# A layer handover rearranged at five places: VectorE work in parts, output products between state sums, one table load placed by hand

## What is computed

```python
x = x + _L0_xattn_ref(_layernorm(x), ctx_4096, ...)  # both operands quantised to 8 bit codes, then one matmul
x = x + _L0_attn_ref(_layernorm(x), ...)             # state space layer: W_in, conv, scan, gate, W_out
x = x + _L0_ffn_ref(_layernorm(x), ...)              # W_base and a routed low-rank sum of 8 experts
x = x + _L1_xattn_ref(_layernorm(x), ctx_4096, ...)  # cross attention over 1024 context rows
x = x + _L1_attn_ref(_layernorm(x), ...)             # causal attention, 32 heads, 8 key heads
x = x + _L1_ffn_ref(_layernorm(x), ...)              # permuted columns, per-head up, GELU, down
```

## Time and profile before

| | us |
|---|---|
| median of 3 runs | 383.94 |
| lowest, highest | 383.87, 384.13 |
| profiled execution, device time | 383.87 |
| profiled execution, span of the trace | 382.1 |
| TensorE busy | 346.7 |
| VectorE busy | 271.5 |
| ScalarE busy | 199.0 |
| GpSimd busy | 121.3 |

### The profile page before, as it was taken

The page is one execution under the profiler, slowest core; times in us unless marked ns, Lnnn a source line. Parts: engine busy times, 40 slices in busy tenths (PEclk is TensorE's granted clock), DMA queues, the critical chain, the costliest instruction groups (busy, mean ns, idle before and its releaser), DMA issues.

```text
span 382.1 us, 5181 instructions
## 1 busy us (share of the span) xinstructions
PE 346.7 (91%) x1996; PEld 223.9 (59%) x1996; DVE 271.5 (71%) x352; ACT 199.0 (52%) x397; POOL 121.3 (32%) x96
## 2 busy tenths in 40 slices
PE   0688999999899989999999979799999989899996
PEld 0335444654566656566754857588443467787785
DVE  2867067757887999998975589887820699976381
ACT  1980223179999688688702664554010379252160
POOL 2600000025999888798920020201000020210000
PEclk9999999999999999999999999999999999999999
DMA  6999999563003011166137789399999997000001
GB/s 252 421 424 407 350 422 383 208 218 112 2 1 112 0 60 51 50 211 240 50 107 237 324 333 425 120 334 332 341 420 423 409 421 307 2 3 0 0 3 55
DMA packets 12967, 81.86 MB, mean 214 GB/s; under 512 B 2109, under 2 KB 2365, under 8 KB 3661
## 3 DMA queue, kind: packets, MB, share of 16 engines
q1 hardware_dynamic: 11614, 78.23, 52.9%
q10 hardware_dynamic: 1296, 3.22, 2.5%
q0 software_dynamic: 32, 0.07, 0.0%
HBM read 80.86 MB, written 0.52 MB: 213 GB/s over the span
## 4 chain that ended last, share of the span: by engine, by line
PE 63%; DVE 15%; POOL 10%; DMA 6%; ACT 3%; issue 2%; SPq 0%; DVEq 0%; ACTq 0%; POOLq 0%
PE psum L1021 13%; PE psum L973 10%; PE psum L1141 7%; PE psum L1242 6%; DMA ring<-in_ctx 6%; PE psum L1097 5%; POOL arena L620 5%; PE psum L980 5%; PE psum L935 4%; PE psum L1165 3%; DVE rounded L1646 2%; DVE arena L1603 2%; POOL arena L623 2%; PE psum L1396 2%; PE psum L1361 2%; POOL plain L620 2%
## 5 line engine op out<-in xcount | busy, mean ns | idle before, releaser
L770 ACT ACTIVATE arena<-arena 128x126 f32<-128x126 f32 x256 | 76.5, 388 | 9.8 <-DVE arena L1603 8.8
L1021 PE MATMUL psum<-ring,hT 128*128 128x512 f32 x128 | 60.6, 602 | 0.8 <-ACT hT L686 0.8
L1603 DVE TENSOR_TENSOR_SCAN arena<-arena,psum 128x1024 f32<-128x1024 f32 x24 | 54.2, 2273 | 3.3 <-PE psum L1097 3.0
L560 POOL TENSOR_TENSOR small<-small 128x1 f32<-128x1 f32 x6 | 9.3, 1553 | 133.0 <-DVE small L1446 127.4
L620 POOL TENSOR_TENSOR arena<-arena 128x1024 f32<-128x1024 f32 x20 | 47.2, 2361 | 5.4 <-DVE arena L1603 5.4
L1646 DVE TENSOR_TENSOR rounded<-ring,rounded 128x2048 fp32r<-128x2048 f32 x16 | 36.5, 2286 | 10.2 <-ACT rounded L797 10.1
L1141 PEld LDWEIGHTS psum<-arena,ident 128*128 128x128 f32 x292 | 35.6, 192 | 13.8 <-issue 10.0
L797 ACT ACTIVATE rounded<-ring 128x2048 fp32r<-128x2048 f32 x16 | 30.6, 1912 | 24.8 <-PE psum L980 15.3
L1141 PE MATMUL psum<-arena,ident 128*128 128x128 f32 x292 | 37.3, 278 | 1.5 <-POOL arena L623 1.5
L1021 PEld LDWEIGHTS psum<-ring,hT 128*128 128x128 f32 x128 | 22.2, 190 | 27.1 <-issue 26.0
L1097 PE MATMUL psum<-plain 64*128 64x512 f32 x128 | 36.1, 641 | 1.7 <-DVE arena L1603 1.4
(11 more groups left out here) (213 smaller groups left out, 581.2 us busy)
## 6 DMA issues: line engine op xcount, KB each, us to landing
ring<-in_w_in SPq DMA_DIRECT2D x16, 1024.0 KB, 14.1
ring<-in_ctx SPq DMA_DIRECT2D x13, 1024.0 KB, 11.9
ring<-in_w_out SPq DMA_DIRECT2D x8, 1024.0 KB, 4.8
ring<-in_ctx_t SPq DMA_DIRECT2D x7, 1024.0 KB, 6.4
ring<-in_w_base SPq DMA_DIRECT2D x4, 1024.0 KB, 4.8
ring<-in_x_wk SPq DMA_DIRECT2D x4, 1024.0 KB, 7.9
ring<-in_a_wo SPq DMA_DIRECT2D x4, 1024.0 KB, 10.9
ring<-in_x_wq SPq DMA_DIRECT2D x3, 1024.0 KB, 8.9
```

Of the source, the lines that this page charges most:

```text
L770: last = act.activation(to, of, ACT.Exp, scale=a_par[:, k, state_no:state_no + 1])
L1021: last = pe.matmul(psum[:, proj_bank(j), :], hT[:, k, :], slot(w_in + u)[:, k % UK, :], start=(k == 0), stop=(k == KT - 1))
L1603: dve.tensor_tensor_scan(state[s % STATES], dA[:, s % 3, :], psum[:, p:p + 2, :].rearrange("p a b -> p (a b)"), 0.0, ALU.mult, ALU.add).th ...
```

## The change

- `context_offset(0)` goes between `code(4)` and `code(5)`, `add_to_x(0, 0)` between `code(5)` and `code(6)`. In unit 7 the last two query products are issued after the last two column sums, with a signal of their own (`q_done` now counts to 3).
- `statistics(0)` goes from `add_to_x` to `variance`, in all handovers.
- `low(5)`, `low(9)`, `low(17)` become two halves (`low_part`), one ahead of `left_low` and one behind it, both ahead of `variance`.
- `low(16)` goes ahead of both `add_to_x`; on ACT `high(17)` goes ahead of `left_high(hT_psum, 8)`.
- Three `output` products stand behind each of `state_sum(29)`, `state_sum(30)`, and the rest behind the last, in place of two, two and the rest.
- The idle products ahead of the second layer's transposes are 5 instead of 11.
- ACT's table for GELU is loaded behind the last `left_high`, ahead of the copy of `picked`.

```diff
-            pool.wait_ge(q_done, 2)
+            pool.wait_ge(q_done, 3)
...
             high(16)
+            high(17)
             left_high(hT_psum, 8)
-            high(17)
             high(18)
...
             left_high(hT_psum, 10)
+            act.preload_act_table_set("gelu_and_others")
             act.wait_ge(g_psum, 1)
...
-                            pe.matmul(psum[rows, nh, :], q1T[:, UK * kh + k, rows], right, **at)
+                            if u < 7 or k < UK // 2:
+                                pe.matmul(psum[rows, nh, :], q1T[:, UK * kh + k, rows], right, **at)
                             last = pe.matmul(psum[rows, 2 + nh, :], ones64, right, **at)
                 last.then_inc(q_done, 1)
+            for k in range(UK // 2, UK):
+                last = pe.matmul(psum[L:P, 1, :], q1T[:, UK + k, L:P], q2[:, 7, UN * k:UN * k + UN], start=False,
+                                 stop=(k == UK - 1))
+            last.then_inc(q_done, 1)
...
-            idle_products(4, 11)
+            idle_products(4, 5)
             transpose_h(1)
...
             state_sum(STEPS - 3)
-            output(0, 0)
-            output(0, 1)
+            for k in range(3):
+                output(0, k)
             state_sum(STEPS - 2)
-            output(0, 2)
             output(0, 3)
+            output(1, 0)
+            output(1, 1)
             state_sum(STEPS - 1)
-            for k in range(GD):
-                output(1, k)
+            output(1, 2)
+            output(1, 3)
...
                 dve.wait_ge(x_ready, updates[0])
-                if nh == 0:
-                    statistics(0)
...
             def variance(n):
 
+                statistics(0)
                 statistics(1)
...
             code(4)
+            dve.wait_ge(x_offset, 1)
+            context_offset(0)
             code(5)
+            add_to_x(0, 0, q_s12)
             code(6)
             code(7)
-            dve.wait_ge(x_offset, 1)
-            for nh in range(2):
-                context_offset(nh)
-                add_to_x(nh, nh, q_s12)
+            context_offset(1)
+            dve.wait_ge(q_done, 3)
+            add_to_x(1, 1, q_s12)
...
+            def low_part(m, part):
+
+                dve.wait_ge(unit_high, m + 1)
+                unit = unit_halves[m % 3]
+                v = slice(2 * part, 2 * part + 2)
+                last = dve.tensor_tensor(unit[:, 1, v, :], slot(split_units[m])[:, v, :], unit[:, 0, v, :].bitcast(F32),
+                                         ALU.subtract)
+                if part:
+                    last.then_inc(unit_low, 1)
...
             center()
+            low_part(5, 0)
             left_low(2)
+            low_part(5, 1)
             variance(2)
-            low(5)
             low(6)
...
             for nh in range(2):
-                if nh == 1:
+                if nh == 0:
                     low(16)
                 dve.wait_ge(xatt_psum, nh + 1)
                 add_to_x(nh, 2 + nh, sinv)
```

More of the change, by code:

```diff
@@ L1699, in _ @@
             center()
+            low_part(9, 0)
             left_low(4)
+            low_part(9, 1)
             variance(3)
-            low(9)
             low(10)
@@ L1756, in _ @@
             center()
+            low_part(17, 0)
             left_low(6)
+            low_part(17, 1)
             variance(4)
-            low(17)
             low(18)
```

## The result

| | median us | lowest to highest | profiled execution | span |
|---|---|---|---|---|
| before | 384.01 | 383.87 to 384.13 | 383.87 | 382.1 |
| changed | 379.04 | 379.00 to 379.14 | 379.14 | 377.2 |

The ratio is 0.9871, with a 95% interval from 0.9857 to 0.9885. The change makes the kernel 5.0 us faster; the forecast was 378.8 with a range from 377.7 to 380.6. The page of the changed kernel answers to the earlier trace rows: VectorE's work fell by 0.9 us and TensorE's by 1.5 (idle products that are gone), so some 3.4 of the 4.9 us of span are time in which TensorE had stood still.

A forecast was written before the change was run, and what follows sets the result against it. TensorE, busy 346.7 of 382.1 us, was taken as the bound, with gains where it stands still. Terms 1.38 + 0.82 + 1.16 + 0.95 + 0.86 = 5.17 us, so 383.94 - 5.17 = 378.8; range 377.7 to 380.6.

The forecast's parts named there:

- Step 1: Quantised layer: earlier last column sum lets the second half's context_offset(1) start at 30.32 instead of 31.70; gain 1.38 us.
- Step 2: Output products: a third output fills TensorE's 0.66 us of idling for GpSimd before the state sum; gain 0.82 us.
- Steps 3 and 4: Routed layer and cross attention's projections: halved low parts remove TensorE's waits at units 5 and 9; gains 1.16 and 0.95 us.
- Rival (a): Split handovers: TensorE keeps only VectorE's lead (0.35, 0.35, 0.6), total gain 3.5 us, time 380.4; chance 0.10.
- Step 5: Attention: low(16) ahead of both additions (0.22) and the halved low(17); ScalarE's high(21) late next; gain 0.86 us in all.
- Step 6: Last layer: the moved GELU table load wins 0, since TensorE's first products cover it and release GELU.
- (c): Attention's first unit lands by the DMAs' own clock, total gain only 1.1 us, time 382.8; chance 0.03.
- (d): TensorE falls to 1.2 GHz in shortened idling before the second layer; 30 us of projections slow, 408.8 us; chance 0.02.
- (e): Whole kernel: the edits move nothing that counts, time 383.9; chance 0.01.

The follow-up runs named there:

- e1: Kernel before with only the quantised layer's part (reordered additions and query products, this handover's statistics in variance, 5 idle products): 382.65 us against 384.03.
- e2: Kernel before with only the output products moved, three behind each of two state sums: 383.13 us, ratio 0.9978.
- e3: Kernel before with only the halved low parts at units 5, 9 and 17 and high(17) ahead of left_high; statistics(0) and low(16) unmoved: 379.25 us.
- e4: Changed kernel with statistics(0) put back between the two additions in all handovers but the first: 376.95 us, ratio 0.9823.
- e10: e4 with ScalarE's high(21) moved ahead of the copies of V: 376.67 us, ratio 0.9813 to before.
- e9: Changed kernel with low(16) put back between the two additions before attention: 378.91 us, ratio 0.9870 to before.
- e8: Changed kernel with the GELU table loaded where it was before, behind the copy of gT: 378.93 us against the changed kernel's 379.04.
- e5: Changed kernel without the second addition's wait for the first addition: 378.82 us, ratio 0.9864 to before.
- e12: Changed kernel with 3 instead of 5 idle products ahead of the second layer's transposes: 379.17 us, ratio 0.9887 to before.
- e7: Changed kernel with no idle products ahead of the second layer's transposes: 381.85 us, ratio 0.9947 to before.

## Where the prediction held and where it did not

The shifts of the same instructions from before to the changed kernel, in the order of the prediction:

| step | predicted | measured | where read |
|---|---|---|---|
| 1 quantised layer | 1.38 | 1.28, later 1.25 | transposes 34.06 to 32.78, state sum 189.52 to 188.27 |
| 2 output products | 0.82 | 0.85 | first split product, 2.10 earlier |
| handover to the routed layer | 0 | -0.12 | transposes, 1.98 earlier |
| 3 routed layer | 1.16 | 1.24 | experts' transpose 236.83 to 233.61, 3.22 earlier |
| handover to cross attention | 0 | -0.13 | transposes, 3.09 earlier |
| 4 projections | 0.95 | 0.96 | score transposes, 4.05 earlier |
| 5 attention | 0.86 | 0.86 | unit 21 322.10 to 317.19, 4.91 earlier |
| 6 last layer | 0 | -0.08 | end 378.94 to 374.11, 4.83 earlier |

**Step 1.** Right in its mechanism. Its size is 0.1 off because the last column sum ends at 29.11 + 1.25 = 30.36, not at 30.28. Most of that is scatter: `code(4)`, ahead of the first moved addition, starts 0.07 later already (21.18 and 21.25). The path behind it is unchanged (30.41 to 32.78 is 2.37, where 2.36 stood). That the scan would pass it on was the uncertain part; e1 shows that it does. The DMA to which the prediction tied VectorE's first step of the convolution, "which does not move", did move: VectorE goes on there at 43.78 instead of 44.52.

**Step 2.** Right, alone too (e2). Only a remark beside it misreads the rows: unit 2's low part was ready 8.8 us before its product (205.50 to 214.32), not 4.

**Steps 3 and 4.** The waits named as next late came at the places and in the sizes given: 0.5 for the experts against 0.47, 0.7 for unit 10 against 0.61. The reason given, one more statistics on VectorE, is shown by e3 and e4, in which both waits are absent. What the prediction did not do was to price that statistics by itself. It is in the numbers, as a reduced gain of each step, but no sentence says that the change's second edit costs 2.1 us of what its third gives. Rival (a) is the same mechanism at full strength and fell: VectorE was late in both places, but TensorE's slack took the rest.

**Step 5.** The total is right, and one part of it has a second cause that the prediction did not see. I took 0.22 us for the second addition from `low(16)` having moved. The addition did come 0.15 earlier than the shift before it (301.64 to 297.44 is 4.20, against 4.05). But either of two edits alone lets it go: `low(16)` moved with the statistics in place (e10, 0.04 behind the product), or the statistics moved with `low(16)` in place (e9, 0.05). The change makes both, and pays for the second with the statistics behind. ScalarE's `high(21)` was late next, as put (from 312.89 in the changed kernel), and e10 takes half of that wait away.

**Step 6.** Right: GELU is released by TensorE (e8).

**The shortfall.** The sum was 5.17; the end of the trace came 4.83 earlier, the profiled executions differ by 4.73 and the medians by 4.97. In the traces 0.34 us are missing. The term that was left out is in the handovers: I put their second addition at 0.04 us behind TensorE's product, "the second addition waited for TensorE there anyway: nothing". It waited, but with the statistics gone it carries two waits where it had one, and starts 0.10 to 0.12 behind. e5 shows the cause by taking one wait away (0.22 us by the medians). With the 0.13 of step 1 that is about the difference; errors of up to 0.08 in the other steps, of either sign, cancel. That the medians lie only 0.20 from the sum is scatter: the profiled execution of before was the fastest of its four, that of the changed kernel the slowest. The lower end of the range, 377.7, does not follow from its own words: half of what lay between the values of steps 3 to 5 and their better ends is 0.76, which gives 378.0.

**The other rivals.** (c) did not come in the changed kernel, whose ScalarE rounds unit 16 from 290.46, released by TensorE. e4's trace shows that the mechanism exists and costs 1.2 us when the unit lands two microseconds later than in e10. (d) did not come with 0.67 us of idling, came in one run of four with 1.11 (e12) and in all four with 1.98 (e7). Its price was far off: not 30 us of projections at the low clock but some 3.3 us of them in e7's trace, and a loss of 1.7 to 3.9 us over its four runs. (e) fell.

## What to carry to other kernels

When a cover is taken away from one wait, ask of every short step that was in its shadow what it costs in its new place: 0.61 us of statistics behind a wait of VectorE were free, and the same 0.61 us three times on the path, with the second wait that came of it, were 2.1 us of the 7.1 that the other edits gain. A change of several edits should be measured edit by edit; three of these alone (7.06 us) promise more than all together (4.97), and that gap pointed to the one to undo. Before an engine's filler work is cut, find out how long it may stand still: taking away the last five idle products moved nothing forward here and cost 2.8 us, and with three left one run in four still lost 1.6.

## What the runs showed of the hardware

- **A second semaphore wait on an instruction** delays its start by 0.06 to 0.08 us although its semaphore was reached long ago: 0.12 against 0.04 us behind TensorE's product at one handover (changed kernel and e5), and likewise at three more.
- **TensorE's clock** fell after 1.98 us of idling, 1.1 us of transposes and 0.83 us of idling, to 0.54 as a mean over the next 3.3 us; after 1.11 or 0.67 us in the first place, with the rest alike, the traces show 1.00. It is not the same each time: one of four runs with the 1.11 us has the mean clock and the span of e7's trace (0.995, 378.9 us), and three of four of e7's have a lower mean, 0.991.
- **The landing of attention's first unit** differs from one execution to the next: issued at 278.31 in both, it lets ScalarE start at 289.47 in e10 and at 291.53 in e4. Where its low part is ahead of the additions, that can reach the end (378.10 against 376.88 to 376.96).
